# Four graph layers on one core: attention over sources that gathers node features and turns them, and a first attention with turned one-hots

## What is computed

```python
# layer 0: attention over targets, 4 heads of 16
g = leaky_relu(xl[src] + xr[dst] + edge_attr @ W_e, 0.2)
alpha = segment_softmax(einsum(g, att), dst)
out = segment_sum(xl[src] * alpha, dst) + bias          # then batch norm, gelu
# layer 1: maximum over targets of relu([x_i, x_j - x_i] @ W1 + b1) @ W2 + b2
# layer 2: attention over sources, one head, then a GRU cell
h = relu(concat([x[src], edge_weights, x[dst]]) @ W_att1.T + b_att1)      # 144 wide
alpha = segment_softmax(h @ W_att2.T + b_att2, src)
msg = segment_sum(alpha * (x @ W_lin.T + b_lin)[dst], src)
# layer 3: sum over sources of relu(x[dst] + edge_attr_64), then an MLP
```

## Time and profile before

| | |
|---|---|
| median of three runs | 25,825.76 us |
| the profiled execution | 25,656.45 us, its span 25,654.3 us |
| PE, DVE, POOL, ACT busy | 74%, 65%, 63%, 26% of the span |
| sort | until about 1,050 us |
| loop of layer 0 | 1,312 to 9,116 us |
| loop of layer 1 | 9,498 to 15,345 us |
| tables of layer 2 | 15,407 to 15,647 us |
| loop of layer 2 | 15,672 to 20,670 us |
| GRU cell | 20,699 to 21,038 us |
| loop of layer 3 | 21,112 to 25,229 us |

### The profile page before, as it was taken

How to read it: one execution, slowest core, us unless ns; L and a number is a source line. 1 busy time by engine, 2 the same in 40 slices (tenths; PEclk the granted TensorE clock), 3 DMA queues, 4 the chain that set the end, 5 groups by cost and what they waited for, 6 DMA issues and landing times. The chain is left out here.

```text
span 25654.3 us, 556495 instructions
## 1 busy us (share of the span) xinstructions
PE 19085.9 (74%) x100300; PEld 12086.3 (47%) x100301; DVE 16571.8 (65%) x59093; ACT 6762.4 (26%) x22440; POOL 16256.9 (63%) x16941
## 2 busy tenths in 40 slices
PE   3578888888888859999999987888888863333334
PEld 1244444444444435555555654666666633333332
DVE  4878888888888864444444556777777654444444
ACT  0033333333333322222222213444444311111111
POOL 0067777777777727777777643666666617777772
PEclk7755555555555555555555557999999855555555
DMA  7032332222233423333333365888888823333332
GB/s 300 5 62 57 57 57 57 57 57 57 57 57 57 57 37 75 76 75 76 75 75 76 70 51 95 132 131 131 129 132 132 117 35 59 59 59 59 59 59 22
DMA packets 3333220, 1984.04 MB, mean 77 GB/s; under 512 B 2469132, under 2 KB 2942196, under 8 KB 3325904
## 3 DMA queue, kind: packets, MB, share of 16 engines
q1 hardware_dynamic: 2735346, 1137.99, 22.6%
q0 software_dynamic: 597808, 845.34, 20.4%
HBM read 1667.63 MB, written 342.49 MB: 78 GB/s over the span
## 5 line engine op out<-in xcount | busy, mean ns | idle before, releaser
L861 POOL DMA_INDIRECT H<-tab,t_idx x3520 | 3405.6, 967 | 2300.0 <-DMA t_ea<-eap 1227.6
L1212 POOL DMA_INDIRECT H<-tab,a_rs x3520 | 3374.7, 959 | 1965.0 <-issue 1193.7
L1571 POOL DMA_INDIRECT H<-tab,m_idx x3520 | 3350.1, 952 | 1654.6 <-issue 1014.7
L1751 POOL DMA_INDIRECT g_G<-tab,g_rs x3232 | 3054.1, 945 | 1520.4 <-issue 944.5
L1495 POOL DMA_INDIRECT rec<-PT,posi x3125 | 3059.9, 979 | 1460.2 <-issue 1224.4
L1817 PE MATMUL g_ps_a<-g_zr,g_oh 128*128 128x64 f32 x6464 | 1586.4, 427 | 2620.3 <-ACT g_zr L1801 2011.6
L1817 PEld LDWEIGHTS g_ps_a<-g_zr,g_oh 128*128 128x128 f32 x6464 | 1438.7, 327 | 2768.6 <-issue 1903.5
L919 DVE CUSTOM_DVE_ANT_0 t_junk<-t_ps_lb,t_pen 128x512 bf16<-128x512 f32 x3520 | 2292.3, 689 | 555.9 <-PE t_ps_lb L1007 257.3
L1007 PE MATMUL t_ps_lb<-t_lgT,t_sel 4*128 4x512 bf16 x3520 | 1894.7, 603 | 498.5 <-DVE t_gm L919 468.6
L1671 PEld LDWEIGHTS m_ps_a<-m_Sx,H 128*128 128x128 f32 x7040 | 1565.6, 327 | 1416.0 <-issue 1415.3
L1035 PEld LDWEIGHTS t_ps_a<-t_V,H 128*128 128x128 f32 x7040 | 1567.5, 328 | 1367.1 <-issue 1367.1
(11 more groups left out here) (344 smaller groups left out, 37049.3 us busy)
## 6 DMA issues: line engine op xcount, KB each, us to landing
a_rs<-rec SPq DMA_DIRECT2D x880, 164.0 KB
rec<-H SPq DMA_DIRECT2D x46, 3116.0 KB
g_rs<-rec SPq DMA_DIRECT2D x3232, 41.0 KB
t_row<-key SPq DMA_DIRECT2D x880, 128.0 KB
m_row<-key SPq DMA_DIRECT2D x880, 128.0 KB
H<-startp SPq DMA_DIRECT2D x880, 128.0 KB
a_row<-keyc SPq DMA_DIRECT2D x880, 128.0 KB
PT<-in_ea SPq DMA_DIRECT2D x625, 160.0 KB
```

Of the source, the lines that this page charges most:

```text
L861: pool.indirect_dma_start(G[:, k, t, :], None, table, bass.IndirectOffsetOnAxis(ap=idx[:, k, t, :], axis=0)).then_inc(s_g[k], 16)
L1212: pool.indirect_dma_start(G[:, k % SLOTS, t, 0:R], None, tab2, bass.IndirectOffsetOnAxis(ap=rs[:, k, t, 1:2], axis=0)).then_inc(s_g[k % SL ...
L1571: pool.indirect_dma_start(G[:, k, t, :], None, tab1, bass.IndirectOffsetOnAxis(ap=idx[:, k, t, :], axis=0)).then_inc(s_g[k], 16)
L1751: pool.indirect_dma_start(G[:, k, t, :], None, tab3, bass.IndirectOffsetOnAxis(ap=rs[:, k, t, 1:2], axis=0)).then_inc(s_g[k], 16)
```

## The change

The tile rows of the sort are stored from ACT's queue and no longer from SP's.

In the loop of layer 0, DVE writes the edges-down one-hot once, in bf16 (`ohb`). PE turns it, and ACT makes three tiles of it: `ohN` and the penalty `pen` from the turned one in PSUM, and the float32 `oh` from `ohb`. The broadcast load of keys and DVE's one-hot from it are gone. Scores and new maxima are carried as two bf16 parts, so DVE has a `split` and two small operations on `mn` more, `edge_maxima` has 8 matmuls for 4, and the score rows are copied without a change of order.

In the loop of layer 2, POOL gathers the 64 node features themselves from `tab3` into 8 buffers. ACT puts the 16 edge features beside them, PE turns this tile of 81 columns (one is the constant 1) four times a group, ACT copies it, and PE multiplies it by the 144-column weights. DVE's scores read PSUM directly, with no add. `keep_busy` and its bank are gone. `node_tables` makes 144 columns in place of 352 and stores none. The linear map is folded into the weights of the GRU, whose product has 320 columns in place of 256 and which has a short prologue for it.

The core of the diff (the scores' cap of 70 also becomes 1, and `M` starts at another constant):

```diff
-                        sp.wait_ge(s_ti, c + 1)
+                        act.wait_ge(s_ti, c + 1)
                         for o in range(2):
-                            sp.dma_start(tiles[o:o + 1, a:b], ti[0:1, c % 2, o, 0:b - a]).then_inc(s_tst[c % 2], 16)
-                    sp.wait_ge(s_rec, 16 * n_rec)
-                    sp.wait_ge(s_eap, 16)
+                            act.dma_start(tiles[o:o + 1, a:b], ti[0:1, c % 2, o, 0:b - a]).then_inc(s_tst[c % 2], 16)
...
-                        def onehots(g, k, r):
-                            at_least(dve, s_me, g - SLOTS + 1)
-                            at_least(dve, s_pen, g - SLOTS + 1)
-                            settle(dve)
-                            dve.tensor_scalar(ohN[:, k], row[:, k], base_node[:, 0, bass.ds(g, 1)], pcol[:], ALU.subtract, ALU.is_equal).then_inc(s_ohN, 1)
+                            dve.tensor_scalar(lo[:], key[:, k, :, 0], base_node[:, order, bass.ds(g, 1)], None, ALU.subtract).then_inc(s_lo, 1)
+
+                        def onehot(g, k, r):
+                            q = k % 2
                             dve.wait_ge(s_lo, g + 1)
-                            at_least(dve, s_acc, g - SLOTS + 1)
-                            for t in range(T):
-                                ins = dve.tensor_scalar(oh[:, k, t, :], iota_b[:], lo[:, t:t + 1], None, ALU.is_equal)
+                            at_least(dve, s_ohT, g - 1)
+                            at_least(dve, s_oh32, g - 1)
+                            for t in range(T):
+                                ins = dve.tensor_scalar(ohb[:, q, t, :], iota_b[:], lo[:, t:t + 1], None, ALU.is_equal)
                             ins.then_inc(s_oh, 1)
...
+                        def split(g, k, r):
+                            dve.wait_ge(s_lp0, g + 1)
+                            dve.tensor_tensor(lgp[:, :, 1, :], lg[:, k % 2], lgp[:, :, 0, :], ALU.subtract).then_inc(s_lp, 1)
...
-                            settle(dve)
                             dve.tensor_tensor(mn[:], m_old, gm[:], ALU.max).then_inc(s_mn, 1)
                             dve.wait_ge(s_mn, g + 1)
+                            at_least(dve, s_me, g)
+                            dve.tensor_copy(mnp[:, 0], mn[:]).then_inc(s_mh, 1)
                             at_least(dve, s_corr, g)
                             dve.tensor_tensor(df[:], m_old, mn[:], ALU.subtract).then_inc(s_df, 1)
                             dve.wait_ge(s_df, g + 1)
                             dve.tensor_tensor(m_old, mn[:], mn[:], ALU.max).then_inc(s_mb, 1)
+                            dve.wait_ge(s_mh, g + 1)
+                            dve.tensor_tensor(mnp[:, 1], mn[:], mnp[:, 0], ALU.subtract).then_inc(s_ml, 1)
 
...
+                            q = k % 2
+                            pe.wait_ge(s_oh, g + 1)
+                            at_least(pe, s_pen, g)
+                            for t in range(T):
+                                mm = pe.transpose(ps_oh[:, t, :], ohb[:, q, t, :], identb[:])
+                            mm.then_inc(s_ohT, 1)
...
-                            pe.wait_ge(s_mn, g + 1)
+                            pe.wait_ge(s_mh, g + 1)
+                            pe.wait_ge(s_ml, g + 1)
                             at_least(pe, s_d0, g)
                             for t in range(T):
-                                mm = pe.matmul(ps_m[:, t * heads:(t + 1) * heads], tile_of(ohN[:, k], t), mn[:], start=True, stop=True)
+                                for i in range(2):
+                                    mm = pe.matmul(ps_m[:, t * heads:(t + 1) * heads], ohN[:, k, t, :], mnp[:, i], start=(i == 0), stop=(i == 1))
...
-                        def penalty(g, k, r):
-                            act.wait_ge(s_ohN, g + 1)
-                            at_least(act, s_gm[heads - 1], g - 1)
-                            act.activation(pen[:, k % 2], ohN[:, k], ACT.Copy, bias=-LOW, scale=LOW).then_inc(s_pen, 1)
+                        def copies(g, k, r):
+                            q = k % 2
+                            act.wait_ge(s_ohT, g + 1)
+                            at_least(act, s_me, g - SLOTS + 1)
+                            act.copy(ohN[:, k], ps_oh[:, 0:T]).then_inc(s_ohN, 1)
+                            at_least(act, s_gm[heads - 1], g - SLOTS + 1)
+                            act.activation(pen[:, k], ps_oh[:, 0:T], ACT.Copy, bias=-BIG, scale=BIG).then_inc(s_pen, 1)
+                            at_least(act, s_acc, g - SLOTS + 1)
+                            act.wait_ge(s_oh, g + 1)
+                            act.copy(oh[:, k], ohb[:, q]).then_inc(s_oh32, 1)
...
                         def score_rows(g, k, r):
                             act.wait_ge(s_lT, g + 1)
                             at_least(act, s_lb[heads - 1], g)
-                            act.copy(lgT[:].rearrange("h (p t) -> h t p", t=T), ps_lT[0:heads, 0:GE].rearrange("h (t p) -> h t p", t=T)).then_inc(s_lTc, 1)
+                            act.copy(lgT[:], ps_lT[0:2 * heads, 0:T * P]).then_inc(s_lTc, 1)
...
-                            at_least(pool, s_acc, g - SLOTS + 1)
+                            at_least(pool, s_acc, g - U + 1)
                             settle(pool)
                             for t in range(T):
-                                pool.indirect_dma_start(G[:, k % SLOTS, t, 0:R], None, tab2,
-                                                        bass.IndirectOffsetOnAxis(ap=rs[:, k, t, 1:2], axis=0)).then_inc(s_g[k % SLOTS], 16)
+                                pool.indirect_dma_start(G[:, k, t, 0:D], None, tab3,
+                                                        bass.IndirectOffsetOnAxis(ap=rs[:, k, t, 1:2], axis=0)).then_inc(s_g[k], 16)
...
                             dve.wait_ge(s_z, g + 1)
-                            dve.wait_ge(s_g[k % SLOTS], uses(k, r) * (16 * T))
-                            at_least(dve, s_sum, g)
-                            settle(dve)
-                            dve.tensor_tensor(z[:].rearrange("p (b t) c -> p b t c", b=2),
-                                              ps_z[:, :, 0:tpb * width].rearrange("p b (t c) -> p b t c", t=tpb),
-                                              G[:, k % SLOTS, :, 0:width].rearrange("p (b t) c -> p b t c", b=2), ALU.add).then_inc(s_act, 1)
-                            dve.wait_ge(s_act, g + 1)
+                            at_least(dve, s_sum, g * 2)
                             at_least(dve, s_lg, g)
                             at_least(dve, s_hi, g)
                             settle(dve)
                             for t in range(T):
-                                ins = dve.scalar_tensor_tensor(z[:, t, :], z[:, t, :], 0.0, att, ALU.max, ALU.mult, accum_out=ss[:, t:t + 1])
-                            ins.then_inc(s_sum, 1)
+                                ins = dve.scalar_tensor_tensor(z[:, t, :], zv[t // tpb][:, t % tpb, :], 0.0, att, ALU.max, ALU.mult, accum_out=ss[:, t:t + 1])
+                                if t % tpb == tpb - 1:
+                                    ins.then_inc(s_sum, 1)
...
-                            at_least(pe, s_eaT, g)
+                            pe.wait_ge(s_g[k], (r + 1) * (16 * T))
+                            at_least(pe, s_gT, g)
                             settle(pe)
-                            pe.transpose(ps_ea[0:T * DE, 0:P], ea[:, k % SLOTS], ident[:]).then_inc(s_eaP, 1)
+                            for t in range(T):
+                                mm = pe.transpose(ps_t[0:GW, t * P:(t + 1) * P], G[:, k, t, :], ident[:])
+                            mm.then_inc(s_t, 1)
...
-                            pe.wait_ge(s_eaT, g + 1)
-                            at_least(pe, s_act, g)
+                            pe.wait_ge(s_gT, g + 1)
                             for b in range(2):
-                                pe.matmul(ps_z[:, b, 0:tpb * width], eaT[:, k % 2], w[:, b * tpb:(b + 1) * tpb, :].rearrange("p t c -> p (t c)"),
-                                          start=True, stop=False)
+                                at_least(pe, s_sum, g * 2 - 1 + b)
+                                for t in range(b * tpb, (b + 1) * tpb):
+                                    pe.matmul(zv[b][:, t % tpb, :], gT[:, k % 2, t * P:(t + 1) * P], w[:], start=(t % tpb == 0), stop=False)
...
-                        def keep_busy(n):
-
-                            for _ in range(n):
-                                pe.matmul(ps_w[:], identb[:], PT[:, 0, 0:3, :].rearrange("p s c -> p (s c)"), start=True, stop=True)
-
                         def body(*at):
-                            keep_busy(1)
                             stage(feature_rows, -1, NG, *at, unroll=U)
-                            stage(turn, -2, NG, *at, unroll=U)
-                            keep_busy(1)
                             stage(spread, 0, NG, *at, unroll=U)
                             stage(key_rows, -1, NG, *at, unroll=U)
```

(13 more changed lines are left out.)

394 lines of the change are left out of this document (247 added, 147 removed).

## The result

The kernel after took 24,781.5 us in the median of four runs (24,774.96 to 24,794.25), the kernel before 25,822.3 beside it: a ratio of 0.9598, 95% interval 0.9581 to 0.9614. That is 1,041 us faster.

What follows compares the result with a forecast made beforehand. Bounds: DVE's store wait in the sort, DVE–PE hand-overs in layer 0's loop, POOL with its DMAs in layer 2's. −200 − 40 − 45 − 490 + 50 = −725 us from the median 25,826: 25,100 us, range 24,830 to 25,620.

Steps and rivals of the forecast that it cites:

- The sort: Sort: with the tile stores on ACT's queue DVE's wait of 210.2 us goes; −200 us, bounds −210 and −100.
- The first attention: Layer 0's loop: DVE relieved, PE's chain becomes the longer; 8.82 us a group for 8.87, −40 us, −250 to +250.
- a loop of hand-overs: Layer 0's loop: neither PE (82% busy) nor DVE (80%) is full; they pass scores and maxima back and forth.
- The first rival: Layer 0's loop: ACT's queued copies make a new wait; 9.41 us a group, +475 us, total 25,615; chance 0.12.
- Tables: Layer 2's node_tables: loses the copy of 208 columns and its store; −45 us, between −30 and −70.
- GRU: GRU cell: a pass of 320 columns for 256, plus 10 us for the prologue; +50 us, between +20 and +70.
- Source attention: Layer 2's loop: POOL's smaller gathers set the pace; 5.10 us a group for 5.66, −490 us, −590 to −250.
- the 4.94 and the 5.14: Layer 2's loop: us a group for POOL's four gathers, with layer 3's issue time (0.29) and today's (0.34).
- The DMA share: Layer 2's loop: falls from 0.83 to about layer 0's 0.32, as the gathers' bytes fall to 31%.
- PE's sum: Layer 2's loop: PE's hot work a group after the change, 5.3 us at most and 4.9 likely.
- The clock: Layer 2's loop: PEclk stays 0.9 or above; rival: falls without keep_busy, 7.6 us a group, 27,300 us, chance 0.11.
- so I take the difference from the median: Whole kernel: −725 us applied to the runs' median of 25,826, not the profiled 25,656, giving 25,100.

Runs made afterwards that it cites:

- e4: Kernel before with DVE's loads of block numbers moved ahead of the one-hots in the first attention: 25,449 us against 25,652, ratio 0.9919.
- e3: Kernel before without its four products a group into the unread bank (keep_busy): 26,395 us against 25,652, ratio 1.0287.
- e10: Kernel before with each of its four unread products replaced by two float32 transposes, eight a group: 25,636 us against 25,666, ratio 0.9991.
- e18: Kernel before with each of its four unread products replaced by one float32 transpose, four a group: 25,728 us against 25,676, ratio 1.0022.
- e12: Kernel after with empty records naming one of 80 node rows in place of row 0: 24,598 us against the kernel after's 24,778.
- e15: Kernel after with two of the four gathers a group left out of layer 2's loop: 24,169 us, 609 less than the kernel after.
- e5: Kernel after, unchanged, on a chip with stalls: 35,792 us, ratio 1.0072 to the kernel before there.

## Why the prediction was wrong

**The sort** was right in mechanism and size: −208 for −200.

**The first attention** had the right picture (a loop of hand-overs, with PE's chain the longer one) and a wrong size, −222 for −40. The step that failed is a missing term: the gap of 0.90 us of the earlier trace rows was read as a sign of a loop of hand-overs and got no line in the sum, though it stood in one group of four and made that group 0.8 us longer. What it was made of can be seen only among the instructions that don't count as busy. The table by place in the unrolled four shows that its leaving the path was 180 of the 222 us, and e4 that the same loads, moved, give 203 us without any of the rest. What remains, 44 us, is about the −40 of the sum. That is partly luck: the sum charged PE 0.14 + 0.6 us of new work and the hand-over 0.4 more, and PE's busy time rose by only 0.1 us a group (6,384.8 us in the 7,804 of the earlier trace rows, 6,490.9 in the 7,600 above, so 7.27 of 8.89 and 7.37 of 8.63). The range for this term, −250, did hold it. The first rival (a new wait behind ACT's copies) fell.

**Tables** −47 for −45, **GRU** +28 for +50: the wider product costs 0.29 us a block more with the prologue, and the sum had 0.42 a block and 10 us for the prologue. **Layer 3's loop** −28: not in the sum; it comes with the stores.

**Source attention** −406 for −490, by a mean over two parts. The 5.66 us of before that I divided were 5.54 in 800 groups and 7.1 in 80. The 800 gained 0.51 us each (410 us), to 5.02, between the 4.94 and the 5.14 worked out from the earlier trace rows; the 80 gained nothing, where the sum had 45 us for them, and their 7.1 us stay in the mean of after, which is 5.2 and not 5.10. The DMA share was wrong: 0.75 and not near a third. Layer 0's loop was taken as the model, where SP's loads (q1) have 17.8%; in this loop they had 36% before and have 47.4% after. And the gathers' queue fell from 46.0% to 27.4%, less than their bytes, which fell to 31%. PE's sum was added up wrongly: its own terms give 5.34 to 5.64 us hot, and not 5.3 at most. It did no harm, since PE's bursts overlap: it was busy 4.43 us a group (3,545 over 800).

**The clock** stayed, so the forecast's side was right, but not by the reason that it gave: PE is busy 88% of the first 800 groups and not 95%, and a busy share of 96% doesn't hold the clock in e3 (0.59). The transposes, which I had taken as a risk, hold it in the kernel before (e10, e18). To have been right here was in part luck, and the chance of 0.11 was, if anything, low for a mechanism that took 743 us in e3.

**The base** took the forecast out of its range. Of the 316 us missed, 156 are the stages'. The other 160 came from the step "so I take the difference from the median", a median that lay 169 us off the profile; the kernel after took 24,780 in both sets, and nothing of the 169 us. Made against the profile, the same sum gives 24,931, with a range from 24,661, which holds 24,780. I had no row that explained the 169 us, and shifted by them without widening the range.

## What to carry to other kernels

List what an engine's sequencer does between two waits, register loads too: a load behind a semaphore wait on the same engine can be on the path when the wait is, and moving it up cost nothing here (e4, −203 us). Where a loop is unrolled, take its time by place in the unrolling, for one group of four can be the long one. Cut a loop into parts before dividing it by its count, and look for groups whose gathers all read one row. Where a profiled execution and the median differ by more than the effect that matters, give the forecast from the profile and put the difference into the range.

## What the runs showed of the hardware

Gathers in which nearly all 128 partitions read one row of memory are slow: the last 80 groups took 6.84 us each, with 66.7% of the DMA engines' time for the queue. With 20 different rows in a gather, 80 in a group, they took 5.02 and 24.9% (e12).

TensorE had two clocks for nearly the same busy share: it was busy 96% of the loop at 0.59 (e3) and 95% at 1.00 (e15). In the kernel before, four transposes a group more took it from 0.59 to 0.91, with PE busy 85% (e18).

Chips differ in what they add to long loops. On two of them the kernels took over 35,000 us; in e5 engines stood at fixed places of each loop, POOL 10 us, PE and ACT 5 to 8, with no releaser that the profile shows (start, us, idle before):

```profile
6000.04 1.95 PE L1118 MATMUL ps_a<-V,H 128*128 128x68 f32 x8
6001.91 1.00 POOL L1584 DMA_INDIRECT rec<-PT,posi  x1 [10.15 <-issue]
...
6013.12 0.23 ACT L1184 ACTIVATE V<-dd 128x16 f32<-128x16 f32 x1 [7.54 <-issue]
...
6014.20 1.94 PE L1118 MATMUL ps_a<-V,H 128*128 128x68 f32 x8 [5.53 <-issue]
```

The short loops (layer inputs 46 us, the first tables 191, the sort 840) took there what they take elsewhere. What stops the engines in the long ones wasn't settled. On the first of the two the kernel after was 0.7% slower than the kernel before.
